# Delta rule chunks: four heads' columns moved through each head's weights

## The reference, cut to what matters

```python
def step(S, inp):                       # S: [batch, head, 128, 32]
    q_t, k_t, v_t, g_t, b_t = inp
    S = S * jnp.exp(g_t)[..., None, None]
    kv = jnp.einsum('bhk,bhkv->bhv', k_t, S)
    delta = (v_t - kv) * b_t[..., None]
    S = S + jnp.einsum('bhk,bhv->bhkv', k_t, delta)
    o_t = jnp.einsum('bhk,bhkv->bhv', q_t, S)
    return (S, o_t)
```

## Time and profile before

| | |
|---|---|
| median of the runs before | 2839.09 us (2835.13 to 2843.67) |
| profiled execution: its own time | 2832.15 us |
| its span | 2830.4 us |
| mean granted TensorE clock | 0.871 |
| PE busy, share of the span | 2573.3 us, 91% |
| DVE, ACT, POOL busy | 1882.2, 1360.2, 1555.7 us |

### The profile page before, as it was taken

The page is one execution under the profiler, slowest core; times in us unless marked ns, Lnnn a source line. Parts: engine busy times, 40 slices in busy tenths (PEclk is TensorE's granted clock), DMA queues, the critical chain, the costliest instruction groups (busy, mean ns, idle before and its releaser), DMA issues. The chain is left out here.

```text
span 2830.4 us, 101424 instructions
## 1 busy us (share of the span) xinstructions
PE 2573.3 (91%) x42655; PEld 1735.6 (61%) x42655; DVE 1882.2 (66%) x3764; ACT 1360.2 (48%) x2430; POOL 1555.7 (55%) x2926
## 2 busy tenths in 40 slices
PE   6847999998699999999999999999999998699976
PEld 2226888888366666666666666666666666245544
DVE  6852322221378888888888888888888886476624
ACT  4721111111156665566666665665666664235532
POOL 0034333230398778777877787778777774113321
PEclk9975555555599999999999999999999999889977
DMA  1000100100321121212131222122211211000000
GB/s 34 0 17 16 22 16 16 22 16 2 126 56 46 52 64 52 83 47 62 49 89 51 62 57 73 47 67 62 74 47 46 54 50 36 26 2 4 4 2 15
DMA packets 99663, 118.03 MB, mean 42 GB/s; under 512 B 41342, under 2 KB 57742, under 8 KB 98446
## 3 DMA queue, kind: packets, MB, share of 16 engines
q1 hardware_dynamic: 99214, 111.58, 14.5%
HBM read 29.47 MB, written 7.34 MB: 13 GB/s over the span
## 5 line engine op out<-in xcount | busy, mean ns | idle before, releaser
L1760 POOL TENSOR_TENSOR l_rot_a<-l_rot_a,l_rot_b 128x512 f32<-128x512 f32 x384 | 481.9, 1274 | 210.4 <-DVE l_rot_b L1609 210.4
L1247 PE MATMUL l_A<-l_wts,l_H 128*128 128x512 f32 x768 | 399.1, 602 | 17.2 <-DMA l_maskb<-in_l_mask 10.8
L1769 POOL TENSOR_TENSOR l_qk<-l_rot_a,l_rn 128x512 f32<-128x512 f32 x384 | 388.3, 1042 | 21.5 <-POOLq L1807 21.2
L1603 DVE TENSOR_TENSOR l_rot_a<-l_A,l_tab 128x512 f32<-128x512 f32 x384 | 258.8, 674 | 177.2 <-ACT l_sq L1476 155.7
L1482 ACT ACTIVATE l_pT<-l_T 128x512 f32<-128x512 f32 x192 | 106.7, 595 | 427.5 <-PE l_T L1293 427.5
L1476 ACT ACTIVATE l_sq<-l_A 128x512 f32<-128x512 f32 x384 | 229.1, 597 | 123.3 <-PE l_A L1247 121.1
L1609 DVE TENSOR_TENSOR l_rot_b<-l_A,l_tab 128x512 f32<-128x512 f32 x384 | 260.7, 679 | 0.0
L1613 DVE TENSOR_REDUCE l_ss<-l_sq 128x8 f32<-128x512 f32 x384 | 259.1, 675 | 0.0
L1346 PE MATMUL l_T<-ident,l_qk 128*128 128x128 f32 x1536 | 207.5, 277 | 14.5 <-POOL l_qk L1769 10.1
L1346 PEld LDWEIGHTS l_T<-ident,l_qk 128*128 128x128 f32 x1536 | 172.6, 141 | 77.7 <-issue 56.2
L1352 PEld LDWEIGHTS l_T<-l_oT,l_wts 128*128 128x128 f32 x1536 | 186.3, 192 | 30.8 <-issue 22.1
(11 more groups left out here) (356 smaller groups left out, 5555.4 us busy)
## 6 DMA issues: line engine op xcount, KB each, us to landing
l_vw<-l_vn SPq DMA_DIRECT2D x384, 128.0 KB
l_vw<-l_vn SPq DMA_DIRECT2D x360, 64.0 KB
l_wts<-in_l_wts SPq DMA_DIRECT2D x18, 650.0 KB, 5.0
c_lower_out<-c_amt SPq DMA_DIRECT2D x16, 384.0 KB, 3.2
l_tab<-in_l_tables SPq DMA_DIRECT2D x6, 1024.0 KB, 5.3
l_wts<-in_l_wts SPq DMA_DIRECT2D x6, 635.5 KB, 4.3
c_inv<-c_bx SPq DMA_DIRECT2D x96, 8.0 KB
result<-x SPq DMA_DIRECT2D x4, 256.0 KB
```

The source lines that it names most:

```text
L1247: pe.matmul(A[j % 2][:], cols(m), w_of(m)[:, C_QKV + 512 * j:C_QKV + 512 * j + 512], start=True, stop=True).then_inc(pq_done, 1)
L1603: dve.tensor_tensor(rot_a[p][:, j, :].rearrange("p (a d) -> p a d", d=DH), src.rearrange("p (a d) -> p a d", d=DH), table[:, a, t:t + 1, : ...
L1760: pool.tensor_tensor(rot_a[m % 2][:, j, :], rot_a[m % 2][:, j, :], rot_b[:, j, :], ALU.add).then_inc(rot_rdy, 1)
L1769: pool.tensor_tensor(qk[:, j, :].rearrange("p (a d) -> p a d", d=DH), rot_a[p][:, j, :].rearrange("p (a d) -> p a d", d=DH), rn[p][:, 8 * ...
```

## The change

The matmuls of `from_state`, `solve` and `to_state` move 128 columns (`WIDE` = 4 heads) in place of 32 and write 128 columns of `s_ps`. The first 32 are the head's own; the other 96 are products of this head's weights with the next three heads' columns. Heads are taken in rising order, so that a later head overwrites what is surplus. The last head reads columns past the sixth head, for which `state`, `rhs`, `xs` and `xd` get three heads more, and its surplus lands past the region or in one written later. For this `from_state` takes all keys before all queries, and `to_state` runs all six `amt` products first (groups 0 and 1) and the six `kn` products last (group 2), which alone now wait for `kn_rdy`. The number of matmuls is unchanged.

```diff
--- before.py
+++ after.py
@@ -188,6 +188,7 @@
 SERIES = range(15, 1, -2)
 GATE_G = 13 + len(SERIES)
 AMT = 4
+WIDE = 4
 
 
 def delta_inputs(nc, ident, xnT, qT, kT, vT, gate, beta, rinv, decay, weights):
@@ -443,7 +444,7 @@
         bx = [sb(f"c_bx{i}", [PROBS, BLK, BLK]) for i in range(2)]
         bt = sb("c_bt", [PROBS, BLK, BLK])
         lower_out = [nc.dram_tensor(f"c_lower_out{i}", (GH, P + 1, P), F32).ap() for i in range(2)]
-        state = [sb(f"c_state{i}", [P, GH, HV]) for i in range(BATCH)]
+        state = [sb(f"c_state{i}", [P, GH + WIDE - 1, HV]) for i in range(BATCH)]
 
         def carved(at, n, width):
             return spare[:, at:at + n * width].rearrange("p (h v) -> p h v", h=n)
@@ -451,9 +452,9 @@
         kn = carved(0, GH, P)
         bv = [carved(GH * P + VD * i, GH, HV) for i in range(2)]
         out = [carved(GH * P + VD * (2 + i), GH, HV) for i in range(2)]
-        rhs = carved(GH * P + VD * 4, GH, HV)
-        xs = carved(GH * P + VD * 5, GH, HV)
-        xd = sb("c_xd", [P, GH, HV])
+        rhs = carved(GH * P + VD * 4, GH + WIDE - 1, HV)
+        xs = carved(GH * P + VD * 5, GH + WIDE - 1, HV)
+        xd = sb("c_xd", [P, GH + WIDE - 1, HV])
 
         low_ps = ps("c_low", [P, 512])
         left_ps = ps("c_left", [P, 512])
@@ -648,27 +649,33 @@
                 if p == 0 and m >= 1:
                     pe.wait_ge(s_rdy, m)
                     pe.wait_ge(o_rdy, m)
-                for h in (2 * p, 2 * p + 1):
-                    for a in range(2):
-                        mm = pe.matmul(s_ps[:, VD * a + HV * h:VD * a + HV * h + HV], kqT[:, a, h, tokens(m)], state[b][:, h, :],
-                                       start=True, stop=True, skip_group_check=True)
+                for i in range(4 * p, 4 * p + 4):
+                    a, h = divmod(i, GH)
+                    c = VD * a + HV * h
+                    mm = pe.matmul(s_ps[:, c:c + WIDE * HV], kqT[:, a, h, tokens(m)], state[b][:, h:h + WIDE, :],
+                                   start=True, stop=True, skip_group_check=True)
                 mm.then_inc(po_done, 1)
 
             def solve(m, a):
                 pe.wait_ge(r_rdy, m + 1)
                 pe.wait_ge(ttf_rdy, m + 1)
                 for h in range(HALF * a, HALF * a + HALF):
-                    mm = pe.matmul(s_ps[:, HV * h:HV * h + HV], invT[m % 2][:, h, :], rhs[:, h, :], start=True, stop=True,
+                    mm = pe.matmul(s_ps[:, HV * h:HV * h + WIDE * HV], invT[m % 2][:, h, :], rhs[:, h:h + WIDE, :], start=True, stop=True,
                                    skip_group_check=True)
                 mm.then_inc(x_done, 1)
 
             def to_state(m, p):
                 pe.wait_ge(x_rdy, m + 1)
-                pe.wait_ge(kn_rdy, 2 * m + 2)
-                for h in (2 * p, 2 * p + 1):
-                    pe.matmul(s_ps[:, VD + HV * h:VD + HV * h + HV], kn[:, h, :], xd[:, h, :], start=True, stop=True, skip_group_check=True)
-                    mm = pe.matmul(s_ps[:, HV * h:HV * h + HV], amt[m % AMT][:, h, 1, :], xs[:, h, :], start=True, stop=True,
-                                   skip_group_check=True)
+                if p < 2:
+                    for h in range(HALF * p, HALF * p + HALF):
+                        mm = pe.matmul(s_ps[:, HV * h:HV * h + WIDE * HV], amt[m % AMT][:, h, 1, :], xs[:, h:h + WIDE, :],
+                                       start=True, stop=True, skip_group_check=True)
+                else:
+                    pe.wait_ge(kn_rdy, 2 * m + 2)
+                    for h in range(GH):
+                        c = VD + HV * h
+                        mm = pe.matmul(s_ps[:, c:c + WIDE * HV], kn[:, h, :], xd[:, h:h + WIDE, :], start=True, stop=True,
+                                       skip_group_check=True)
                 mm.then_inc(od_done, 1)
 
             pe.wait_ge(const_ld, 64)
@@ -789,15 +796,15 @@
                 dve.wait_ge(x_done, 2 * m + 2)
                 if m >= 1:
                     dve.wait_ge(od_done, PAIRS * m)
-                dve.tensor_copy(xs, x)
-                dve.tensor_tensor(xd[:], x, per_head(fade, m, HV), ALU.mult).then_inc(x_rdy, 1)
+                dve.tensor_copy(xs[:, 0:GH, :], x)
+                dve.tensor_tensor(xd[:, 0:GH, :], x, per_head(fade, m, HV), ALU.mult).then_inc(x_rdy, 1)
 
             def advance(m):
                 b = place(m)[0]
                 dve.wait_ge(od_done, PAIRS * m + PAIRS)
                 dve.wait_ge(s_dec, m + 1)
                 dve.wait_ge(r_rdy, m + 1)
-                dve.tensor_tensor(state[b][:], heads(s_ps, HV, GH, VD), state[b][:], ALU.add).then_inc(s_rdy, 1)
+                dve.tensor_tensor(state[b][:, 0:GH, :], heads(s_ps, HV, GH, VD), state[b][:, 0:GH, :], ALU.add).then_inc(s_rdy, 1)
                 dve.tensor_tensor(out[m % 2], heads(s_ps, HV, GH), out[m % 2], ALU.add).then_inc(o_rdy, 1)
 
             def take_values(m):
@@ -862,6 +869,7 @@
             for i in range(2):
                 dve.memset(invT[i][:], 0.0)
             dve.memset(u4[:], 0.0)
+            dve.memset(xd[:], 0.0)
             dve.memset(upper[:], 0.0)
             dve.tensor_scalar(minus[:], decay[:, 0], -1.0, None, ALU.mult)
             dve.reciprocal(unnorm[:], r_k).then_inc(small_rdy, 1)
@@ -931,7 +939,7 @@
                 pool.wait_ge(po_done, PAIRS * m + PAIRS)
                 if m >= 2:
                     pool.wait_ge(s_rdy, m - 1)
-                pool.tensor_tensor(state[b][:], state[b][:], per_head(decay[:, 2], m, HV), ALU.mult).then_inc(s_dec, 1)
+                pool.tensor_tensor(state[b][:, 0:GH, :], state[b][:, 0:GH, :], per_head(decay[:, 2], m, HV), ALU.mult).then_inc(s_dec, 1)
 
             def gated(m):
                 t = place(m)[1]
```

## The result

The changed kernel takes 2651.48 us (median, 2647.01 to 2656.54) against 2837.11 in the same comparison: ratio 0.9343, 95% interval 0.9319 to 0.9368. The prediction was 2654 us. Its profiled execution has a span of 2650.8 us against 2830.4 and a mean granted clock of 0.942 against 0.871.

The account below looks back on a forecast made before the run. PE at half clock (1.2 GHz) was taken to bound the chunk stage; savings of 149 us in steady units, 11 in the first and 25 in the tail, together 185, take the median from 2839.1 to 2654 us, range 2630 to 2722.

Parts of the forecast that it names:

- The clock follows the streamed columns and not the busy time: Chunk stage: streams of wide records raise PE's clock and hold it at 1.00; records of 32 columns let it fall.
- second rival: Chunk stage: the clock ignores the added columns; only the wait for ACT's key copy goes, 11 us: 2828 us; 6%.
- 128 columns cost nothing behind a load of 128 weights: State products: the load sets the pace, 96 further columns are free; 60 records at 0.120 take 7.2 us at full clock.
- The 0.162 us a record: State products: alternative cost from the skill's 81 ns pair, two passes; 2.5 us more a step, sum some 35 us higher.
- third rival: State products: clock stays at half and wide records cost 0.12 us more, like the output product's: 2943 us; 4%.
- The other 18.1 us at the ratio 0.54: Levels, `products`, `decays` and transposes of a step: shrink to 9.8 us at full clock, making the step 17.0 us.
- First unit and tail: Ends of the chunk stage: first unit takes 20 us, saving 11; last 86.0 us become 61.4, saving 25.
- the last step from the profile to the median: Whole run: profiled 2832.15 us, 7 under the median, would take 2647; the median of 2839.1 becomes 2654 us.
- The wait for the keys: Before `to_state`: PE's 0.67 us wait for ACT's key copy goes, because the `amt` products run first.
- SP's loop: SP's chain from weighing through transfers and `build` to `lower4`: needs 17.0 us and just fits the step.
- fourth rival: Steady units: SP's chain binds at 18 to 19 us, 15 to 30 us less gain, 2669 to 2684; 77% together with the forecast.
- The signs: Chunk stage: clock 0.95 or more, units 16.5 to 18 us apart, POOL's and DVE's waits for `from_state` roughly halved.

Follow-up runs that it names:

- one head's columns: The changed kernel with WIDE at 1 instead of 4, so each matmul moves its own 32 columns in the new order: 2833.65 us, ratio 0.9999.
- the padding: The changed kernel with zero rows bringing the output stage's second matmul of each token block from 64 to 128 rows: 2633.85 us, ratio 0.9289.

## Why the prediction was right

**The clock follows the streamed columns and not the busy time.** Right, and shown from both sides: narrow records with PE busy for 100% of 338 us stay at 0.50 (one head's columns), wide ones hold 1.00 for 11 units, and narrowing 24 of the 60 brings relapses a microsecond behind the narrow ones. The second rival, in which the clock does not care for the added columns, is refuted. The Trainium skill (TensorE: Matmul & The Clock Gate, Part 1: The HAM clock gate) says that the clock follows how busy PE has recently been. If busy is read as the busy time of a trace, the run with one head's columns disagrees: 338.00 of 338.00 us busy, at 0.50. Whether it is the columns or what goes with them (operands read, results written) no run separates. That 64 columns hold what they do not soon raise was no part of the prediction.

**128 columns cost nothing behind a load of 128 weights.** Right at half clock (3.52 against 3.62 us for 16). At full clock the term was 7.2 us and measured 7.09. Against 64 columns a unit is 0.21 to 0.25 us longer, which may be the longer drain at the end of each group; that was not isolated. The 0.162 us a record, an estimate from the Trainium skill (TensorE: Matmul & The Clock Gate, Back-to-back issue gap), did not come: 0.118. The third rival's row was explained by the padding.

**The other 18.1 us at the ratio 0.54.** This term was a little small: 9.8 us predicted, and 17.59 less 7.09 leaves 10.5. `lower4` (488.75 to 489.51 before, 0.76 us) still takes 0.53 us, 372.11 to 372.64, a ratio of 0.70: these tiny tiles gained less from the clock than the rest. The unit came to 17.59 us instead of 17.0, so the steady units gave 142.8 us instead of 149.

**First unit and tail.** 19.0 us instead of 20, and 58.4 instead of 61.4, with two relapses for the four assumed. Both give back some of the 6.5 us that the steady units lacked, 1 and 3 us; the sum, 182.4 against 185, is nearer than its largest term, which is luck. So is the last step from the profile to the median: the two profiled runs differ by 179.6 us (2832.15 and 2652.6), 5 less than forecast, but the one before was 5 us under its comparison's median and the one after 1 us over, and the medians differ by 185.6.

**The wait for the keys.** The step that said what becomes of it was right for the changed kernel (no wait on ACT is left) but the second rival priced it at 11 us at half clock, and there, as one head's columns show, taking it out is worth nothing in the time (2833.65 against 2833.61 us), since the short rises of the clock went with it. Put back at full clock it costs 9 us in the stage.

**SP's loop.** It was to just fit in 17.0 us. In the changed kernel DVE waits for it and PE does not. DVE's waits from 250 to 530 us:

```profile
DVE c_ic L834 <- DMA c_inv<-c_bx: 8.9, 8, 2.9
```

In the steady units alone it is at most 1.4 us. PE is busy for 99.5% of them and never waits for `build` there, so the fourth rival's mechanism exists but had no price. Whether it would bind in a shorter unit was not tried.

**The signs, and one reading.** The granted clock from 256 us to the stage's end is 0.99 (0.95 or more was forecast), a unit takes 17.5 to 18.0 us, and DVE's waits for `from_state` in the eleven units fell from 50.0 to 26.7 us, about half as forecast, POOL's from 136.0 to 35.9, to a quarter. The run of fives in the clock of the earlier trace rows spans the fourth to the eleventh slice, and PE is busy there at 6 to 9 tenths, not at 8 or 9 from the third on as the prediction reads it; nothing in its sum hangs on this, since the times come from the earlier trace rows.

## What to carry to other kernels

Where PE is busy and its granted clock is at half, look at what the matmuls move: here float32 matmuls with 128 by 128 weights took as long with 32 columns as with 128 (0.226 and 0.22 us a record at half clock), and the added columns brought the clock up for everything around them. Widening is worth most where the clock has to be raised; a clock that is up is held with less. In such a stretch every other wait is worth measuring again afterwards, since those for other engines do not shrink with it (ACT's copy: 0.49 us at either clock). And where weights of 64 and 128 rows take turns, padding with zero rows can be faster than leaving the rows out.

## What the runs showed that was not expected

- One and the same program can differ by 79 us from run to run (64 columns), which fits a clock that stands just at the edge of rising; with 128 columns in the first `from_state` alone it was 8 us.
- A PE without any gap, at half clock for 338 us, was no faster than one with a wait in every unit and a few short rises of the clock: 2833.65 and 2833.61 us.
- A record cost 0.13 us more at half clock where 64-row and 128-row weights took turns (0.34 against 0.21 from start to start), and 64 added zero rows, with the rise of the clock that came with them, took 18 us off the run.
